# Conditioning of batch 1 begun before the attention units: minimum on GpSimd, exponentials and first scans ahead, the rest at other places

## What is computed

```python
# conditioning of x: k = v = f (fside), r = x
ek = exp(min(f, 30)); ekv = ek * f
nf, df = forward scans over t of (ekv, ek):  a = a * decay + in
nb, db = the same scans backward
euk = exp(min(u + f, 30))
num = nf + nb - ekv + euk * f
den = df + db - ek + euk
out = sigmoid(r) * num / max(den, 1e-8) * (0.8 + 0.2 * tf)

x = x + attention(cond(x), W_K, W_Q, W_V, W_O)      # 16 heads of 128
x = x + experts(cond2(x), gate_w, expert_w, expert_b)  # top 2 of 8
```

## Time and profile before

| | us |
|---|---|
| median of 3 runs | 371.82 |
| lowest, highest | 371.78, 371.84 |
| the profiled execution | 371.82 |
| its span, first to last instruction | 369.9 |

### The profile page before, as it was taken

How to read it: one execution, slowest core, us unless ns; L and a number is a source line. 1 busy time by engine, 2 the same in 40 slices (tenths; PEclk the granted TensorE clock), 3 DMA queues, 4 the chain that set the end, 5 groups by cost and what they waited for, 6 DMA issues and landing times.

```text
span 369.9 us, 7426 instructions
## 1 busy us (share of the span) xinstructions
PE 344.7 (93%) x2404; PEld 319.4 (86%) x2404; DVE 318.7 (86%) x892; ACT 255.9 (69%) x687; POOL 212.6 (57%) x223
## 2 busy tenths in 40 slices
PE   0796599999999999999999999999999989899997
PEld 0685499998999999989999999999999979788885
DVE  4979899999898989899989999999768576869675
ACT  5669888788878869886888888878778565321100
POOL 1875686855756468867867886787673424210000
PEclk9999989999999999999999999999999999999999
DMA  5670130100000000130100022100000000000000
GB/s 166 240 276 4 57 113 2 59 4 1 2 0 3 1 2 0 52 123 0 28 31 3 1 73 101 58 3 1 2 2 1 2 1 2 0 16 15 28 28 30
DMA packets 4613, 14.13 MB, mean 38 GB/s; under 512 B 848, under 2 KB 1888, under 8 KB 3936
## 3 DMA queue, kind: packets, MB, share of 16 engines
q1 hardware_dynamic: 4352, 13.66, 11.0%
q10 hardware_dynamic: 224, 0.01, 0.0%
HBM read 12.60 MB, written 1.05 MB: 37 GB/s over the span
## 4 chain that ended last, share of the span: by engine, by line
PE 63%; DVE 28%; ACT 3%; issue 3%; DMA 1%; DVEq 0%; ACTq 0%
PE psQK L947 7%; PE psQK L949 7%; PE psQK L948 7%; DVE tiles L729 4%; PE psT L1017 4%; PE psO L947 3%; PE psS L947 3%; PE psS L949 3%; PE psS L948 3%; PE psO L949 3%; PE psO L948 3%; PE psV L947 3%; PE psS L1003 3%; PE psZ L1030 3%; PE psV L948 3%
## 5 line engine op out<-in xcount | busy, mean ns | idle before, releaser
L324 POOL TENSOR_SCALAR prob<-prob,rsum 128x256 f32<-128x256 f32 x60 | 55.5, 925 | 63.1 <-DVE rsum L764 63.1
L947 PE MATMUL psQK<-y_hi,w_hi 128*128 128x256 f32 x256 | 72.2, 282 | 1.1 <-DVE y_lo L679 1.1
L518 ACT ACTIVATE prob<-prob,ntop 128x256 f32<-128x256 f32 (+1 forms) x128 | 57.0, 448 | 23.1 <-DVE ntop L756 23.0
L949 PE MATMUL psQK<-y_hi,w_lo 128*128 128x256 f32 x256 | 72.3, 282 | 0.0
L948 PE MATMUL psQK<-y_lo,w_hi 128*128 128x256 f32 x256 | 72.2, 282 | 0.0
L330 POOL TENSOR_TENSOR z_lo<-z_lo,z_two 128x256 fp32r<-128x256 f32 x64 | 48.2, 753 | 33.7 <-DVE z_lo L782 33.7
L289 POOL TENSOR_TENSOR w_lo<-raw,w_hi 128x512 fp32r<-128x512 f32 x40 | 53.7, 1352 | 11.2 <-ACT w_hi L383 11.1
L947 PEld LDWEIGHTS psQK<-y_hi,w_hi 128*128 128x128 f32 x256 | 48.6, 190 | 2.9 <-issue 1.5
L948 PEld LDWEIGHTS psQK<-y_lo,w_hi 128*128 128x128 f32 x256 | 48.6, 190 | 1.3
L949 PEld LDWEIGHTS psQK<-y_hi,w_lo 128*128 128x128 f32 x256 | 48.7, 190 | 0.0
L506 ACT ACTIVATE qk<-psQK 128x512 fp32r<-128x512 f32 x64 | 37.6, 587 | 15.1 <-PE psQK L949 14.8
(11 more groups left out here) (166 smaller groups left out, 1039.1 us busy)
## 6 DMA issues: line engine op xcount, KB each, us to landing
raw<-in_weights SPq DMA_DIRECT2D x5, 1024.0 KB, 5.3
raw<-in_weights SPq DMA_DIRECT2D x10, 512.0 KB, 4.2
out<-fT SPq DMA_DIRECT2D x8, 128.0 KB, 1.7
fT<-in_fT SPq DMA_DIRECT2D x2, 256.0 KB, 5.0
xT<-in_xT SPq DMA_DIRECT2D x2, 256.0 KB, 6.8
fT<-in_fT SPq DMA_DIRECT2D x1, 512.0 KB, 6.2
xT<-in_xT SPq DMA_DIRECT2D x1, 512.0 KB, 6.2
temb<-in_temb ACTq DMA_DIRECT2D x1, 1.0 KB, 3.3
```

The costliest lines, as they stand in the source:

```text
L324: pool.tensor_scalar(prob[:, k, P:3 * P], prob[:, k, P:3 * P], rsum[:, k, 1:2], None, ALU.mult).then_inc(shared, 1)
L518: ins = act.activation(prob[:, k, lo:hi], prob[:, k, lo:hi], ACT.Exp, scale=-1.0, bias=ntop[:, k, q:q + 1], accum_out=ssum[:, k, q:q + 1])
L947: pe.matmul(out, ah, bh, start=first and k == 0, stop=False)
L949: ins = pe.matmul(out, al, bh, start=False, stop=last and k == n - 1)
```

## The change

Batch 1's minimum leaves VectorE (it stood between first_y(1) and first_y_low(1)) for GpSimd, behind the first two w_lo parts; its ekv follows behind the fourth. ScalarE makes its exponentials before first_y_high(0), where they stood behind qk_high(1), and sxd behind qk_high(1). VectorE makes the scans xd before qk_low(0). The pieces that are left get other places:

| piece | before | after |
|---|---|---|
| VectorE xd | (0, M) | before the units |
| xn | (0, E) | (0, M) |
| gd | (1, M) | (1, M) |
| gn | (1, E) | (2, M) |
| den | (2, M) | (2, E) |
| r0, r1 | (2, E), (3, M) | (3, M), (4, M) |
| y | (4, M) | (4, E) |
| ScalarE sxd, sxn | (0, E), (1, M) | before the units, (0, E) |
| yhi | (4, E) | (5, M) |
| GpSimd clamp, eukv, num | 1, 3, 4 | 0, 2, 3 |

```diff
-POOL_FIRST = {"ekv": 0, "clamp": 1, "den": 2, "eukv": 3, "num": 4, "y_low": 5}
+POOL_FIRST = {"clamp": 0, "den": 2, "eukv": 2, "num": 3, "y_low": 5}
...
-        for h in range(GH):
-            refill("qk", 0, h)
+
+        def first_min():
+            pool.wait_ge(in_f1, 16)
+            pool.tensor_scalar(tiles[:, 1, EK], cols(fT, 1), LIMIT, None, ALU.min).then_inc(c_dve[1], 1)
+
+        refill("qk", 0, 0)
+        refill("qk", 0, 1)
+        first_min()
+        refill("qk", 0, 2)
+        refill("qk", 0, 3)
+        products(1)["ekv"]()
...
+        cond(1)["exps"]()
         first_y_high(0)
         for part in range(2):
             refill("o", 0, part)
         first_y_high(1)
         qk_high(0)
         qk_high(1)
-        cond(1)["exps"]()
+        cond(1)["sxd"]()
         do(-1, "E")
...
-
-        cond(1)["min"]()
         first_y_low(1)
+
+        cond(1)["xd"]()
         dve.wait_ge(consts, 2 + E)
         qk_low(0)
```

More of the change, by code:

```diff
@@ L57 @@
 POOL_PLACES = {"ekv": -1, "clamp": 2, "den": 3, "eukv": 4, "num": 5, "y_low": 8}
-DVE_FIRST = {"xd": (0, "M"), "xn": (0, "E"), "gd": (1, "M"), "gn": (1, "E"), "den": (2, "M"), "r0": (2, "E"), "r1": (3, "M"), "y": (4, "M")}
-ACT_FIRST = {"sxd": (0, "E"), "sxn": (1, "M"), "e1": (1, "E"), "yhi": (4, "E")}
-POOL_FIRST = {"ekv": 0, "clamp": 1, "den": 2, "eukv": 3, "num": 4, "y_low": 5}
+DVE_FIRST = {"xn": (0, "M"), "gd": (1, "M"), "gn": (2, "M"), "den": (2, "E"), "r0": (3, "M"), "r1": (4, "M"), "y": (4, "E")}
+ACT_FIRST = {"sxn": (0, "E"), "e1": (1, "E"), "yhi": (5, "M")}
+POOL_FIRST = {"clamp": 0, "den": 2, "eukv": 2, "num": 3, "y_low": 5}
 REFILL = {1: (("qk", 0, -1), ("qk", 1, 0), ("v", 0, 1), ("qk", 2, 2), ("v", 1, 2), ("qk", 3, 3), ("o", 0, 5), ("o", 1, 8)),
```

## The result

The changed kernel takes 373.12 us (median of 20 runs, 372.92 to 373.41) against 371.81 us of the kernel before beside it (20 runs, 371.68 to 373.25). The ratio is 1.0035, with a 95% interval from 1.0028 to 1.0041: **slower by 1.3 us**, 0.3 us above the top of the forecast range. The profiled execution's span is 371.2 us; before it was 369.9.

What follows compares the result with a forecast made beforehand. TensorE bounds nearly everywhere, VectorE at the start; VectorE's gains and losses leave +0.1 us at TensorE after 0.17 is swallowed, so span 370.0 plus 1.9 gives 371.9 us, no change; range 370.6 to 372.8.

Steps and rivals of the forecast that it cites:

- What bounds the start: Units 0 to 5: VectorE is late and gapless; a microsecond it gains or loses can reach the end unshortened.
- The rule of scans and GpSimd: Start: two-SBUF-input VectorE instructions and GpSimd tensor_tensor run one after the other; a blocked scan pair takes 2.24 us.
- The xd pair: Ahead of qk_low(0): the scans meet GpSimd's w_lo row, making qk_low(0) start at 22.68 instead of 21.50, +1.17 us.
- Unit 0's xn pair: Unit 0: second scan blocked by w_lo, pair 2.24 us; maxima(1) at 27.97, 0.0 against before.
- Maxima(3): End of unit 2: after gn, den and a minimum meeting w_lo, maxima(3) at 39.42, +0.66 us.
- Units 3 and 4: r0 for r1 changes nothing; r1 for y +0.56, then y +0.6; maxima(5) at 49.2, +1.8 us.
- Unit 5's xd pair: Unit 5: the pair meets an idle GpSimd, 1.26 us instead of 2.78, −1.5; v_lo then +0.27 us.
- rival 2: Unit 4 or 5: one more wait makes v_lo 0.7 to 1.0 later, 372.6 to 372.9 us; chance 0.14.
- Behind it TensorE's waits are few: Behind pT_low(4), 0.9 late on ScalarE's account but ending just before its turn at 55.9: few TensorE waits.
- Rival 1: Unit 0's xn or unit 2's minimum escapes its wait: v_lo 1.0 earlier, 370.8 us; chance 0.24, with clock fall 0.06.
- Rival 3: Clock falling as VectorE leads puts TensorE 0.7 behind, 372.5 us; falling earlier, as TensorE waits, costs nothing; chance 0.08.
- Rival 4: Scans before qk_low(0) not blocked: units 0 to 2 1.2 earlier, later half eaten by ScalarE, 370.6 us; chance 0.06.

Runs made afterwards that it cites:

- e3: Changed kernel with batch 2's minimum moved from the end of unit 2 into VectorE's wait ahead of pT_low(0): 371.74 us against 371.69 before the change.
- e6: Changed kernel with GpSimd waiting for both xd scans ahead of its second w_lo part of v: 371.68 us against 371.69 before the change.
- e9: Changed kernel with batch 1's second reciprocal (r1) moved ahead of pT_low(2) in unit 4, into VectorE's wait: 372.44 us against 371.74 before the change.
- e5: Changed kernel with group 0's two o parts of w_lo moved on GpSimd into units 1 and 3: 372.17 us against 371.77 before the change.
- e7: Changed kernel with one group 1 o-weights part moved from unit 5 to 6 on ScalarE, 6 to 7 on GpSimd: 372.82 us against 371.69 before.
- e10: Changed kernel with the edits of e3, e6, e7 and e9 together: 370.97 us against 371.74 before the change.
- e1: Changed kernel with minimum, exponentials, ekv and first scans still ahead, batch 1's other pieces at their old places: 372.84 us against 371.77 before the change.
- e11: Changed kernel with 14 short, unused y_hi products in TensorE's wait for qk_low(0): 372.97 us against 371.74 before the change.
- e12: e10 plus 8 and 14 short, unused products in TensorE's pT waits of units 3 and 4: 369.23 us against 371.74 before the change.

## Why the prediction was wrong

**What bounds the start** was right: what VectorE gains or loses in units 0 to 5 reaches the end. e3, e6 and e9 moved VectorE by 1.5, 1.4 and 0.8 us and the end by 1.4, 1.4 and 0.7. One thing is to be added: VectorE wasn't without gaps in units 0 to 5. Before the change it stood idle for 1.42 us ahead of pT_low(2), waiting for ScalarE, and such waits are where e3 and e9 found their room.

**The rule of scans and GpSimd** was right, and is now shown by intervention. Scans moved into a gap went from 3.33 to 1.26 us (e6). The clamp-like GpSimd instruction, the minimum at 13.01, took the clamp's 1.49 as forecast.

**The terms.** The xd pair: forecast about 3 us and qk_low(0) at 22.68; measured 3.33 and 22.88, **+1.38 for +1.17**. GpSimd hands over from a w_lo to the minimum and back 0.1 later each time than I let it: 13.01 for 12.91, 14.59 for 14.37. A row of before had it, a clamp starting at 25.77 behind a w_lo that ended at 25.68. As the pair waits for the end of a w_lo, this came through whole. Unit 0's xn pair: 2.31 against 2.24, maxima(1) at 28.13 for 27.97. v_lo of unit 1: 31.77 for 31.62. Maxima(3): 39.75 for 39.42 (**+0.99 for +0.66**), the meeting of the minimum with w_lo being as forecast but for 0.1, on a base already 0.23 late. Units 3 and 4: r1 and y, +1.1 as forecast; maxima(5) 49.55 for 49.2. Unit 5's xd pair: 1.26, as forecast. v_lo: 52.01 for 51.7, so **+0.61 for +0.27**. No mechanism up to here was missing; 0.34 had gathered from steps of 0.1 to 0.2.

**The slack.** The prediction knew that 0.2 us of lateness stood between v_lo and TensorE, and used it for +0.27. At +0.61 TensorE lost 0.46. That is rival 2's deciding point, 0.2 of added lateness in unit 4 or 5, and it was right, while its cause (one more collision in these units) was not what happened: y took 0.74 us and unit 5's pair 1.26. The one more meeting came in unit 6.

**The step that failed** is the sentence "Behind it TensorE's waits are few". It judged a wait from its absence before. I followed pT_low(4), 0.9 late on ScalarE, to its turn, and there it was indeed in time: measured +0.95 (55.19 for 54.24) and no wait. But VectorE goes on from there to z_low(3). Before the change z_low(3) ended at 57.92 and values(4) started at 58.14; as 0.14 us lie between the two where TensorE does wait (59.14 to 59.28), the slack was 0.08. The row was in the trace of before, and I had not read on to it. Together: 0.46 at the projection, 0.09 up to the turn, 0.59 at values(4), 0.07 behind it, make the 1.2 that the maxima of unit 8 show. The first is the mis-sized part (0.1 in the forecast), the third the missed one, and the largest. By my own numbers, pT_low(4) 0.9 late behind a projection 0.1 late, the wait would have been about 0.7 and the forecast 372.6, inside the range but in its upper part.

Where the wait comes from can be read off the versions. From the projection to values(4) TensorE took 5.77 us before and 6.45 after, and 6.45 or 6.46 in e3, e5, e6 and e9 as well, whose projections started between 51.31 and 52.01, earlier than before the change. So it was not the lateness handed on from units 0 to 4. Behind the projection pT_low(4) comes 0.49 later than it did (1.87 us before, 2.36 after), since it waits for ScalarE, whose row without a gap now holds y_hi (0.52 to the next start); the xn pair that meets a w_lo adds 0.27 (1.90 for 1.63 us); less 0.08 of slack that is the 0.68. e7, which takes a w_hi and that meeting away, has 5.83. No run moved y_hi alone, so ScalarE's share is read from the rows and not shown by intervention.

**Rival 1** (a wait missed) didn't happen, but e3 shows its price: the minimum clear of w_lo brought 1.4 us, 0.3 of it its own time, so 1.1 for the 1.0 forecast. **Rival 3** is refuted for the change. The clock fell earlier, "as TensorE waits", and cost nothing, as that rival's second half says. **Rival 4** is refuted by the 3.33.

**The rule of the Trainium skill** (SBUF — State Buffer, section Who interferes with whom) says that a VectorE instruction with two SBUF inputs contends with a GpSimd instruction that reads SBUF, and that a VectorE tensor_scalar, with its one input, can contend with GpSimd too, when it runs in a mode that takes both of VectorE's SBUF ports. For w_lo and the scans the runs agree (3.33 against 1.26). For the clamp the runs differ from the Trainium skill, which has the block last for the whole GpSimd instruction: it held scans up only early in its 1.49 us. The prediction's reading, that the clamp lets scans through, was the later part of that. A scan issued 0.38 us behind the clamp's start took 1.03 us (e5), one 0.24 behind it 0.92 (at 60.28 after the change), one 0.70 behind it 0.69 (at 59.52 in e7), where 0.66 is usual. The minimum of batch 2 on VectorE, which has one input, was kept off (1.49 against 0.36), while a reciprocal with one input took its 1.74 beside GpSimd's tensor_tensor (e9, at 44.29); which mode the minimum ran in no row says. The prediction named no row for it, but the trace of before has one, the minimum of batch 1 beside w_lo parts that start at 17.82 and 19.05:

```profile
18.77 0.61 DVE L697 TENSOR_SCALAR tiles<-fT 128x512 f32<-128x512 f32 x1
```

## What to carry to other kernels

Idle time on an engine is room for an instruction only if the engine that it takes turns with is idle as well (here GpSimd, whose w_lo made a pair of scans take 3.33 us for 1.26): look at both timelines, and make the gap on the less urgent one (e6: 1.39 us of idle GpSimd for 1.4 us of the kernel). When a change makes a chain late, write down for each thing it hands to the bounding engine how long that thing lay ready before, until the lateness has died out, and follow each piece of work that is moved to the next such thing on every engine, not only on the one that is the late one. Small slacks decide (0.17 and 0.08 us here), and a list of the waits of before does not show them. Steps of 0.1 to 0.2 added up to 0.34 by unit 5, twice the slack that the forecast relied on.

## What the runs showed of the hardware

- A minimum with one SBUF input on VectorE waited for a GpSimd tensor_tensor as a scan does: 1.49 us against 0.36, 0.90 in e3 beside eukv, and 0.61 before the change. A reciprocal with one SBUF input did not wait (1.74 us in e9).
- The clamp on GpSimd held a scan up only early in its run: 0.92 and 1.03 us for scans issued 0.24 and 0.38 behind its start, 0.69 for one issued 0.70 behind it.
- GpSimd's change from a w_lo to the minimum or the clamp, or from the minimum to a w_lo, took 0.1 us more than from one w_lo to the next (starts at 13.01 and 14.59). The shares (L324), a tensor_scalar too, show no such step: y_lo from 52.28 for 1.28, the shares at 53.55.
- The mean granted clock differed between executions of one kernel (0.994 to 1.0 in e10), and over the kernels the falls to 0.50 stood in different stretches. What one cost depended on who led: nothing in the change, 0.7 us in e1, 1.6 us in e10. Short products in TensorE's waits kept it at 1.0 (e11 in its stretch, e12 throughout).
- A product of 32-bit values on TensorE, 128x256, stood in the trace as two instructions and took 0.44 us (7.07 for 16, at full clock); a short one of the same shape took 0.13 (1.84 for 14, e11).
